# A three-level wavelet mix on one core: all products of TensorE on two halves of 64 rows, edge rows copied into one operand

## The chip, the core and the metric

The kernel runs on one core of a Trainium2 chip. The time is device time of one execution in microseconds; less is better. A core has TensorE (PE, matrix products into PSUM), VectorE (DVE), ScalarE (ACT), GpSimd (POOL) and SyncE (SP, which issues the DMAs here). They run their own instruction streams and meet at semaphores. SBUF and PSUM have 128 partitions; PSUM has 8 banks of 512 fp32 columns.

## What is computed

x is [8, 512, 207, 64] fp32: batch, time, nodes, channels. Each series of 512 steps is split by a three-level wavelet transform with 8 taps into four components, each component is multiplied by a weight of its channel, the transform is inverted, the 64 channels are mixed by a 64 x 64 matrix, and x and a bias are added:

```python
for _ in range(3):
    a, d = _dwt(a)                      # stride 2, 8 taps, along time
    details.append(d)
coeffs = [a] + details[::-1]
enh = [c * w[i] for i, c in enumerate(coeffs)]      # w[i]: one weight per channel
rec = enh[0]
for d in enh[1:]:
    rec = _idwt(rec[:, :d.shape[-1]], d)
return x + xr @ proj_w.T + proj_b       # xr: rec as [B, T, N, D]
```

## The kernel before

Time is cut into 4 windows of 128 steps, which lie on the partitions of `x_sb`. The three transforms of a window are one matrix: a window gives 128 coefficients of its own, and 20 more (`HALO_COLS`) reach over its edge and belong to the next window. The way back is a matrix too: a window's output needs its own 128 coefficients and the first 20 of the next window (its edge rows). After the last window there is a tail of 20 coefficients that no window owns.

Two nodes of 64 channels make a pair (128 rows or columns), four pairs a group (512 columns). 9 groups make a turn (`turn_of`), 23 turns all the nodes: 207 groups. The first and the last turn are written out, the 21 between run in a loop (`Fori`). Four slots of 18 nodes hold x; SP loads slot k+3 and stores slot k as the sums get done.

For each group the stages are:

- analysis (PE, `analyse`, L364), per pair: 4 products, one a window, with `x_sb` as the weights and the 148-column matrix moving, into the only set of banks `coefs_ps` (2 banks). Each needs the scaling of the pair before (`scaled`).
- scaling (DVE, `scale_pair`, L520): `coefs_ps` times the component weights to `coefs_sb`; POOL adds the 20 coefficients at the seam between windows 1 and 2 (`add_seam`, L311).
- projection (PE, `project`, L389), per window: 4 products, one a pair; the weights are 128 coefficients, the moving operand is `w_sb`, which holds the 64 x 64 matrix twice on its diagonal (128 x 128). Two banks `proj_ps` serve five tiles in turn: windows 0, 1, 2, the tail (`project_tail`, L396) and window 3.
- the split in two numbers of type fp32r: ACT copies the high part (`copy_high`, L493), DVE subtracts it for the low part (`split_low`, L526). The tail comes out transposed, is turned by DVE (`turn_tail`, L536, four instructions) and split by ACT (L498) and POOL (L316).
- synthesis (PE, `synthesise`, L407 to L409), per window: low matrix x high data, high x low, high x high, into its own bank of `synth_ps` (4 banks).
- edges (PE, `synthesise_edges`, L418): the edge rows are taken where they lie, in a block of 32 rows of the next window's tile. Coefficient orders (`OWN`, `ORDER_OF`) are chosen so that the blocks of the four windows are four different ones. Three steps of four products with 32 rows, which run side by side.
- bias and sum: POOL adds the bias to x (`add_bias`, L323), DVE adds the synthesis to it (`add_window`, L546).

PE's order is written out in its `turn_of`: projection of window 0, window 3 of the group behind, analysis of pair 0 of the group ahead, the edges of the group behind, then projection, analysis and synthesis by turns. fp32 products appear in the trace as two instructions each, with a weight load (PEld) each; fp32r products as one.

## Time and profile before

| | us |
|---|---|
| median of 3 runs (2462.97 to 2463.97) | 2463.24 |
| the profiled execution | 2463.63 |
| its span in the trace | 2461.8 |

| engine | busy us | share of the span |
|---|---|---|
| PE, matmuls | 2433.9 | 99% |
| PE, weight loads | 2203.3 | 89% |
| DVE | 1896.4 | 77% |
| POOL | 1473.9 | 60% |
| ACT | 626.5 | 25% |

Busy times of PE are modelled ends of pipelined matmuls: what a matmul costs is read from the distance of two starts, not from its duration. The granted clock of TensorE is 1.00 of 2.4 GHz in the stretches read below. DMA moved 435 MB at 177 GB/s. "<-" names what ended an engine's idle time; "issue" means nothing that the profile shows.

### The profile page before, as it was taken

Reading aid. Unit: us, or ns where it says so; the run is one execution under the profiler, and the core shown is the slowest. Engines: PE = TensorE matmul, PEld = TensorE weight load, DVE = VectorE, ACT = ScalarE, POOL = GpSimd, SP = SyncE. Lnnn points to the kernel's source line nnn. Section 1 sums busy time; section 2 is a strip of 40 time slices with the busy share of each in tenths; the row PEclk is TensorE's granted clock in tenths of the full one; section 3 lists DMA queues with packets and bytes.
Section 4 is the critical chain, followed back from the end, with each engine's and each line's share of the span. In section 5 each row is a group of like instructions: output and inputs, shape, how many; then the busy total and the mean of one; then the engine's idle time right before and its main releaser. Section 6 shows DMA issues by size and latency. Waiting matters only on the chain.

```text
span 2461.8 us, 51862 instructions
## 1 busy us (share of the span) xinstructions
PE 2433.9 (99%) x18630; PEld 2203.3 (89%) x18630; DVE 1896.4 (77%) x3315; ACT 626.5 (25%) x1038; POOL 1473.9 (60%) x1908
## 2 busy tenths in 40 slices
PE   7999999999999999999999999999999999999998
PEld 7999999999999999999999999999999989998987
DVE  4777777777777777777777777777777777777776
ACT  1222222222222222222222222222222222222222
POOL 4656665666656666665666666566665665666555
PEclk9999999999999999999999999999999999999999
DMA  3544454454544544454454544544454454644543
GB/s 129 200 174 179 173 197 153 168 216 153 222 162 153 204 173 177 171 195 153 172 211 153 227 157 153 208 174 177 170 192 157 172 207 153 230 154 153 212 162 128
DMA packets 106160, 435.35 MB, mean 177 GB/s; under 512 B 6288, under 2 KB 7696, under 8 KB 106128
## 3 DMA queue, kind: packets, MB, share of 16 engines
q1 hardware_dynamic: 105232, 434.13, 46.7%
q10 hardware_dynamic: 896, 0.79, 0.1%
q8 instruction: 20, 0.33, 0.1%
q14 instruction: 12, 0.10, 0.0%
HBM read 217.84 MB, written 217.06 MB: 177 GB/s over the span
## 4 chain that ended last, share of the span: by engine, by line
PE 98%; POOL 0%; issue 0%; DVE 0%; DMA 0%; ACT 0%; ACTq 0%; DVEq 0%; POOLq 0%
PE coefs_ps L364 34%; PE proj_ps L389 32%; PE synth_ps L409 8%; PE synth_ps L408 8%; PE synth_ps L407 8%; PE synth_ps L418 8%; PE proj_ps L396 2%; DMA comp_sb<-comp_w 0%; POOL scale_sb L301 0%; POOL tail_lo L316 0%; DVE x_sb L546 0%; DVE coefs_sb L520 0%; DVE proj_lo L526 0%; ACT proj_hi L493 0%; ACTq L166 0%
## 5 line engine op out<-in xcount | busy, mean ns | idle before, releaser
L323 POOL TENSOR_TENSOR x_sb<-x_sb,bias_sb 128x512 f32<-128x512 f32 x828 | 1052.7, 1271 | 5.2 <-issue 5.2
L364 PE MATMUL coefs_ps<-analysis_sb,x_sb 128*128 128x148 f32 x6624 | 975.3, 290 | 12.7 <-DMA analysis_sb<-analysis_m 9.1
L493 ACT ACTIVATE proj_hi<-proj_ps 128x512 fp32r<-128x512 f32 x828 | 494.6, 597 | 1807.1 <-PE proj_ps L389 1807.1
L389 PEld LDWEIGHTS proj_ps<-w_sb,coefs_sb 128*128 128x128 f32 x6624 | 835.3, 192 | 118.1 <-issue 82.8
L364 PEld LDWEIGHTS coefs_ps<-analysis_sb,x_sb 128*128 128x128 f32 x6624 | 895.6, 191 | 32.3 <-DMA analysis_sb<-analysis_m 9.1
L389 PE MATMUL proj_ps<-w_sb,coefs_sb 128*128 128x128 f32 x6624 | 897.5, 278 | 2.3 <-issue 1.6
L526 DVE TENSOR_TENSOR proj_lo<-proj_ps,proj_hi 128x512 fp32r<-128x512 f32 x828 | 573.0, 692 | 422.7 <-ACT proj_hi L493 408.9
L311 POOL TENSOR_TENSOR coefs_sb<-coefs_sb 128x20 f32<-128x20 f32 x828 | 187.2, 226 | 810.1 <-DVE coefs_sb L520 778.8
L520 DVE TENSOR_TENSOR coefs_sb<-coefs_ps,scale_sb 128x552 f32<-128x552 f32 x828 | 600.6, 725 | 86.8 <-PE coefs_ps L364 75.2
L546 DVE TENSOR_TENSOR x_sb<-synth_ps,x_sb 128x512 f32<-128x512 f32 x828 | 531.5, 684 | 32.4 <-PE synth_ps L418 29.7
L407 PE MATMUL synth_ps<-proj_hi,synthesis_lo 128*128 128x512 f32 x828 | 404.0, 488 | 0.7 <-DVE proj_lo L526 0.7
L316 POOL TENSOR_TENSOR tail_lo<-tail_sb,tail_hi 32x512 fp32r<-32x512 f32 x207 | 262.0, 1266 | 154.5 <-ACT tail_hi L498 151.3
L409 PE MATMUL synth_ps<-proj_hi,synthesis_hi 128*128 128x512 f32 x828 | 326.9, 395 | 0.0
L408 PE MATMUL synth_ps<-proj_lo,synthesis_hi 128*128 128x512 f32 x828 | 326.3, 394 | 0.0
L536 DVE STREAM_TRANSPOSE tail_sb<-proj_ps 32x128 f32<-32x128 f32 x828 | 259.6, 313 | 14.9
L409 PEld LDWEIGHTS synth_ps<-proj_hi,synthesis_hi 128*128 128x128 f32 x828 | 155.5, 188 | 35.6
L407 PEld LDWEIGHTS synth_ps<-proj_hi,synthesis_lo 128*128 128x128 f32 x828 | 157.7, 190 | 1.1 <-DVE proj_lo L526 1.1
L408 PEld LDWEIGHTS synth_ps<-proj_lo,synthesis_hi 128*128 128x128 f32 x828 | 157.7, 191 | 0.0
L498 ACT ACTIVATE tail_hi<-tail_sb 32x512 fp32r<-32x512 f32 x207 | 129.9, 628 | 5.2
L418 PE MATMUL synth_ps<-proj_hi,edge_lo 32*128 32x512 f32 x621 | 104.2, 497 | 1.3 <-POOL tail_lo L316 1.3
L418 PE MATMUL synth_ps<-tail_hi,edge_lo 32*128 32x512 f32 x207 | 102.7, 496 | 0.0
L396 PEld LDWEIGHTS proj_ps<-coefs_sb,w_sb 128*128 128x128 f32 x414 | 77.9, 188 | 19.1
(22 smaller groups left out, 644.5 us busy)
## 6 DMA issues: line engine op xcount, KB each, us to landing
out<-x_sb SPq DMA_DIRECT2D x184, 1152.0 KB, 6.0
x_sb<-x SPq DMA_DIRECT2D x182, 1152.0 KB, 11.2
x_sb<-x SPq DMA_DIRECT2D x1, 1024.0 KB, 9.6
x_sb<-x SPq DMA_DIRECT2D x1, 768.0 KB, 6.0
x_sb<-x SPq DMA_DIRECT2D x1, 512.0 KB, 4.2
bias_sb<-bias ACTq DMA_DIRECT2D x1, 256.0 KB, 6.9
analysis_sb<-analysis_m ACTq DMA_DIRECT2D x1, 222.0 KB, 7.0
synthesis_sb<-synthesis_m ACTq DMA_DIRECT2D x1, 192.0 KB, 6.9
```

The source lines that it names most:

```text
L316: nc.gpsimd.tensor_tensor(tail_lo[tail_rows, :], tail_sb[tail_rows, :], tail_hi[tail_rows, :].bitcast(fp32), ALU.subtract).then_inc(tail_l ...
L323: nc.gpsimd.tensor_tensor(cols, cols, bias_sb[:, :], ALU.add).then_inc(biased, 1)
L364: mm = nc.tensor.matmul(coefs_ps[:, w // PART_WINDOWS, AT[w]:AT[w] + COLS], x_sb[:, w, local * PAIR:(local + 1) * PAIR], analysis_sb[:, OR ...
L389: mm = nc.tensor.matmul(ps[:, p * PAIR:(p + 1) * PAIR], coefs_of(g, p)[:, own_cols(w)], w_sb[:, :], start=True, stop=True)
L407: nc.tensor.matmul(rec, lo, proj_hi[w][:, :], start=True, stop=False)
L408: nc.tensor.matmul(rec, hi, proj_lo[w][:, :], start=False, stop=False)
L409: nc.tensor.matmul(rec, hi, proj_hi[w][:, :], start=False, stop=False).then_inc(synthesised, 1)
L418: mm = nc.tensor.matmul(synth_ps[:, w, :], weight[rows, :], moving[w][rows, :], start=False, stop=step == 2)
L493: nc.scalar.activation(proj_hi[w][:, :], proj_ps[BANK[g][TILE_ORDER.index(w)]][:, :], ACT.Copy).then_inc(hi_copied, 1)
L520: nc.vector.tensor_tensor(coefs_of(g, p).rearrange("c (two k) -> c two k", two=PARTS)[:, :, 0:PART_COLS], coefs_ps[:, :, 0:PART_COLS], sca ...
L526: nc.vector.tensor_tensor(proj_lo[w][:, :], proj_ps[BANK[g][TILE_ORDER.index(w)]][:, :], proj_hi[w][:, :].bitcast(fp32), ALU.subtract).the ...
L546: nc.vector.tensor_tensor(cols, synth_ps[:, w, :], cols, ALU.add).then_inc(summed, 1)
```

## The change

A window is cut in two halves of 64 steps, and every product uses 64 of the array's 128 rows; products on the upper and the lower rows follow each other in pairs and write different banks.

- Analysis: 8 products per pair of nodes (4 windows x 2 halves), 64 rows, 84 columns. `analyse_first` has four, `analyse_second` the other four, which add to the same banks and wait for the first (`half_analysed`).
- Projection: one product per node instead of per pair: 64 rows (channels), 64 columns. Each node has its own bank; `proj_ps` is two tiles of two banks. The tail is two products into the free columns of window 3's tile.
- Synthesis: in units of two windows, (2, 3) and (0, 1), which share the two banks of `synth_ps`: `synthesise_first` has six products of 64 rows, `synthesise_second` six more and then the edges.
- Edges: ACT copies the 20 high and the 20 low edge rows of the next window to rows 0 and 32 of a half of `stack_sb` (`move_edge`, `move_tail`), where three rows hold the bias in three parts. Two steps (matrix low part, matrix high part) of two products with 64 rows take the place of three steps of four. The rows above the three bias rows in the matrix hold ones, so POOL's bias additions go away.
- The tail is turned by two transposes of 64 rows and split as 128 x 128 instead of 32 x 512.
- The orders of PE, DVE, ACT and POOL are rewritten; `add_window` waits for a unit (`synthesised`). At the start ACT splits the bias and issues 12 small DMAs into `stack_sb`.

```diff
@@ pe
+            def analyse_half(w, side, start, stop):
+                at = (w % PART_WINDOWS) * WINDOW + side * HALF
+                return lambda cols: nc.tensor.matmul(coefs_ps[:, w // PART_WINDOWS, at:at + HALF_COLS],
+                                                     x_sb[half_rows[side], w, cols], analysis_sb[half_rows[side], :],
+                                                     start=start, stop=stop, skip_group_check=True)
...
+                if not (first and local == 0):
+                    pe.wait_ge(scaled, (turn * GROUPS + g) * PAIRS + p)
+                cols = pair_cols(g, p)
+                analyse_half(0, 0, True, False)(cols)
+                analyse_half(2, 1, True, False)(cols)
+                analyse_half(1, 0, False, False)(cols)
+                analyse_half(3, 1, False, False)(cols).then_inc(half_analysed, 1)
+
+            def analyse_second(turn, g, p):
+                pe.wait_ge(half_analysed, (turn * GROUPS + g) * PAIRS + (p + 1))
+                cols = pair_cols(g, p)
+                analyse_half(2, 0, False, False)(cols)
+                analyse_half(0, 1, False, False)(cols)
+                analyse_half(3, 0, False, True)(cols)
+                analyse_half(1, 1, False, True)(cols).then_inc(analysed, 1)
...
+                for p in pairs:
+                    if w == ORDER[0]:
                         pe.wait_ge(seamed, group * PAIRS + (p + 1))
-                    mm = nc.tensor.matmul(ps[:, p * PAIR:(p + 1) * PAIR], coefs_of(g, p)[:, own_cols(w)], w_sb[:, :],
-                                          start=True, stop=True)
+                    for node in range(2):
+                        out_cols = proj_of(w)[:, node, 0:NODE_COLS].rearrange("k (h p c) -> k h p c", h=2, p=PAIRS)
+                        rows = node_rows[node]
+                        mm = nc.tensor.matmul(out_cols[:, :, p, :], coefs_of(g, p)[rows, own_cols(w)],
+                                              w_sb[rows, rows].rearrange("k (h c) -> k h c", h=2),
+                                              start=True, stop=True, skip_group_check=True)
...
+                for weight, stop in ((edge_lo[:, :], False), (edge_hi[:, 0, :], True)):
+                    nc.tensor.matmul(synth_ps[1][:, :], weight[half_rows[0], :], stack_sb[u][half_rows[0], :],
+                                     start=False, stop=stop, skip_group_check=True)
+                    mm = nc.tensor.matmul(synth_ps[0][:, :], weight[half_rows[1], :], stack_sb[u][half_rows[1], :],
+                                          start=False, stop=stop, skip_group_check=True)
+                mm.then_inc(synthesised, 1)
...
+                    if not start:
+                        synthesise_second(*behind, LATE)
+                    first_ahead(0)
+                    project(turn, g, 2, [0, 1, 2, 3], first)
+                    second_ahead(0)
+                    project(turn, g, 3, [0, 1, 2, 3], first)
+                    project_tail(g)
+                    first_ahead(1)
+                    if not start:
+                        synthesise_first(*behind, EARLY, [0, 1, 2], False)
+                    second_ahead(1)
+                    if not start:
+                        synthesise_second(*behind, EARLY)
+                    first_ahead(2)
+                    project(turn, g, 0, [0, 1, 2, 3], first)
+                    second_ahead(2)
+                    project(turn, g, 1, [0, 1, 2, 3], first)
...
+                    synthesise_first(turn, g, LATE, [0], first)
+                    first_ahead(3)
+                    synthesise_first(turn, g, LATE, [1, 2], first)
+                    second_ahead(3)
@@ act
+            def move_edge(turn, g, w, u, half, first):
+                group = turn * GROUPS + g
+                act.wait_ge(lo_copied, group * WINDOWS + (PLACE[w] + 1))
+                if not (first and g == 0):
+                    act.wait_ge(synthesised, group * 2 + (u - 1))
+                for at, source in ((HIGH_AT, proj_hi[w]), (LOW_AT, proj_lo[w])):
+                    rows = slice(half * HALF + at, half * HALF + at + HALO_COLS)
+                    nc.scalar.activation(stack_sb[u][rows, :], source[0:HALO_COLS, :].bitcast(fp32),
+                                         ACT.Copy).then_inc(edge_moved[w], 1)
...
+                    for q in range(4):
+                        cols = slice(q * PAIRS * QUAD, (q + 1) * PAIRS * QUAD)
+                        nc.scalar.activation(stack_sb[LATE][at:at + HALO_COLS, cols],
+                                             source[q * QUAD:q * QUAD + HALO_COLS, :].bitcast(fp32),
+                                             ACT.Copy).then_inc(tail_moved, 1)
...
+                    if not (first and g == 0):
+                        move_edge(*behind, 2, EARLY, 0, first and g == 1)
+                        move_edge(*behind, 1, EARLY, 1, first and g == 1)
+                    copy_high(turn, g, 2, first)
+                    copy_high(turn, g, 3, first)
+                    move_edge(turn, g, 3, LATE, 1, first)
+                    copy_tail_high(turn, g, first)
+                    move_tail(turn, g, first)
+                    copy_high(turn, g, 0, first)
+                    copy_high(turn, g, 1, first)
@@ dve
+                    if not (first and g == 0):
+                        split_low(*behind, 1)
+                    add_behind(2)
+                    add_behind(3)
                     scale_ahead(0)
+                    split_low(turn, g, 2)
+                    split_low(turn, g, 3)
+                    scale_ahead(1)
+                    turn_tail(turn, g, first)
                     add_behind(0)
                     add_behind(1)
                     scale_ahead(2)
+                    split_low(turn, g, 0)
                     scale_ahead(3)
```

## Rows read from the trace of the kernel before

**Rows 1.** The page, part 1: busy us, share of the span, instructions.

```profile
PE 2433.9 (99%) x18630; PEld 2203.3 (89%) x18630; DVE 1896.4 (77%) x3315; ACT 626.5 (25%) x1038; POOL 1473.9 (60%) x1908
```

**Rows 2.** The page, part 4: the chain that ended last, by line.

```profile
PE coefs_ps L364 34%; PE proj_ps L389 32%; PE synth_ps L409 8%; PE synth_ps L408 8%; PE synth_ps L407 8%; PE synth_ps L418 8%; PE proj_ps L396 2%; DMA comp_sb<-comp_w 0%; POOL scale_sb L301 0%; POOL tail_lo L316 0%; DVE x_sb L546 0%; DVE coefs_sb L520 0%; DVE proj_lo L526 0%; ACT proj_hi L493 0%; ACTq L166 0%
```

**Rows 3.** Waits of PE: total us, times, longest us.

```profile
PE coefs_ps L364 <- DVE coefs_sb L520: 3.7, 3, 1.9
```

**Rows 4.** Groups of instructions: PE's two fp32 lines; busy us, mean ns, idle before.

```profile
L364 PE MATMUL coefs_ps<-analysis_sb,x_sb 128*128 128x148 f32 x6624 | 975.3, 290 | 12.7 <-DMA analysis_sb<-analysis_m 9.1
L389 PE MATMUL proj_ps<-w_sb,coefs_sb 128*128 128x128 f32 x6624 | 897.5, 278 | 2.3 <-issue 1.6
```

**Rows 5.** Weight loads in order of time: start us, length us, line, count.

```profile
37.87 0.82 PEld L364 LDWEIGHTS coefs_ps<-analysis_sb,x_sb 128*128 128x128 f32 x6
38.84 0.19 PEld L418 LDWEIGHTS synth_ps<-proj_hi,edge_lo 32*128 32x128 f32 x3 [0.15 <-issue]
...
38.95 0.19 PEld L418 LDWEIGHTS synth_ps<-proj_lo,edge_hi 32*128 32x128 f32 x3
...
39.18 0.19 PEld L418 LDWEIGHTS synth_ps<-proj_hi,edge_hi 32*128 32x128 f32 x3
...
39.74 0.97 PEld L389 LDWEIGHTS proj_ps<-w_sb,coefs_sb 128*128 128x128 f32 x8 [0.37 <-issue]
40.63 1.06 PEld L364 LDWEIGHTS coefs_ps<-analysis_sb,x_sb 128*128 128x128 f32 x8
...
41.75 0.19 PEld L408 LDWEIGHTS synth_ps<-proj_lo,synthesis_hi 128*128 128x128 f32 x1
41.98 0.19 PEld L409 LDWEIGHTS synth_ps<-proj_hi,synthesis_hi 128*128 128x128 f32 x1
...
109.98 0.30 PEld L389 LDWEIGHTS proj_ps<-w_sb,coefs_sb 128*128 128x128 f32 x2 [0.37 <-issue]
```

**Rows 6.** Groups of instructions of the other engines, as in the fourth group.

```profile
L493 ACT ACTIVATE proj_hi<-proj_ps 128x512 fp32r<-128x512 f32 x828 | 494.6, 597 | 1807.1 <-PE proj_ps L389 1807.1
L526 DVE TENSOR_TENSOR proj_lo<-proj_ps,proj_hi 128x512 fp32r<-128x512 f32 x828 | 573.0, 692 | 422.7 <-ACT proj_hi L493 408.9
L520 DVE TENSOR_TENSOR coefs_sb<-coefs_ps,scale_sb 128x552 f32<-128x552 f32 x828 | 600.6, 725 | 86.8 <-PE coefs_ps L364 75.2
L546 DVE TENSOR_TENSOR x_sb<-synth_ps,x_sb 128x512 f32<-128x512 f32 x828 | 531.5, 684 | 32.4 <-PE synth_ps L418 29.7
L536 DVE STREAM_TRANSPOSE tail_sb<-proj_ps 32x128 f32<-32x128 f32 x828 | 259.6, 313 | 14.9
L498 ACT ACTIVATE tail_hi<-tail_sb 32x512 fp32r<-32x512 f32 x207 | 129.9, 628 | 5.2
L323 POOL TENSOR_TENSOR x_sb<-x_sb,bias_sb 128x512 f32<-128x512 f32 x828 | 1052.7, 1271 | 5.2 <-issue 5.2
...
L483 ACT ACTIVATE edge_hi<-edge_sb 128x128 fp32r<-128x128 f32 x1 | 0.3, 292 | 0.0
```

**Rows 7.** Analysis to scaling, scaling to analysis: PE and DVE in order of time.

```profile
1209.06 1.17 PE L364 MATMUL coefs_ps<-analysis_sb,x_sb 128*128 128x148 f32 x8
...
1210.27 0.73 DVE L520 TENSOR_TENSOR coefs_sb<-coefs_ps,scale_sb 128x552 f32<-128x552 f32 x1 [0.30 <-PE coefs_ps L364]
...
18.94 0.73 DVE L520 TENSOR_TENSOR coefs_sb<-coefs_ps,scale_sb 128x552 f32<-128x552 f32 x1 [2.49 <-PE coefs_ps L364]
...
19.73 2.34 PE L364 MATMUL coefs_ps<-analysis_sb,x_sb 128*128 128x148 f32 x8 [0.82 <-DVE coefs_sb L520]
```

**Rows 8.** DMA queues, and PE's first matmuls of the last turn in time order.

```profile
q1 hardware_dynamic: 105232, 434.13, 46.7%
...
q8 instruction: 20, 0.33, 0.1%
...
2346.85 0.40 PE L418 MATMUL synth_ps<-proj_hi,edge_hi 32*128 32x512 f32 x3
2347.87 0.39 PE L418 MATMUL synth_ps<-tail_hi,edge_hi 32*128 32x512 f32 x1 [0.62 <-issue]
```

More of the change, by code:

```diff
@@ L32 @@
 GROUP = PAIRS * PAIR
-TAIL = WINDOWS
-TILE_ORDER = [0, 1, 2, TAIL, 3]
-TILES = len(TILE_ORDER)
-TAIL_QUAD = 2
+NODE_COLS = GROUP // 2
+ORDER = [2, 3, 0, 1]
+PLACE = [ORDER.index(w) for w in range(WINDOWS)]
+UNITS = [(2, 3), (0, 1)]
+LATE, EARLY = 0, 1
+HIGH_AT, LOW_AT = 0, QUAD
+BIAS_AT = HALO_COLS
+BIAS_PARTS = 3
 SLOTS = 4
@@ new lines, in products, with synthesise_first @@
+            def products(u):
+                low, high = UNITS[u]
+                return [(synthesis_lo, proj_hi[low], proj_hi[high]), (synthesis_hi, proj_lo[low], proj_lo[high]),
+                        (synthesis_hi, proj_hi[low], proj_hi[high])]
+            def synthesise_first(turn, g, u, steps, first):
+                group = turn * GROUPS + g
+                if steps[0] == 0:
+                    pe.wait_ge(lo_copied, group * WINDOWS + (2 * u + 2))
+                    if not (first and g == 0 and u == 0):
+                        pe.wait_ge(summed, group * WINDOWS + 2 * u)
+                for step in steps:
+                    weight, low, high = products(u)[step]
+                    nc.tensor.matmul(synth_ps[0][:, :], weight[half_rows[0], :], low[half_rows[0], :],
+                                     start=step == 0, stop=False, skip_group_check=True)
+                    mm = nc.tensor.matmul(synth_ps[1][:, :], weight[half_rows[1], :], high[half_rows[1], :],
+                                          start=step == 0, stop=False, skip_group_check=True)
+                if steps[-1] == 2:
+                    mm.then_inc(half_synthesised, 1)
@@ L450, in turn_of @@
-                    project(turn, g, 2, first)
-                    analyse_ahead(2)
-                    synthesise(turn, g, 1, first)
-                    project_tail(turn, g, first)
-                    project(turn, g, 3, first)
-                    analyse_ahead(3)
-                    synthesise(turn, g, 2, first)
+                    start = first and g == 0
+                    behind = (turn, g - 1) if g > 0 else (turn - 1, GROUPS - 1)
+                    ahead = (turn, g + 1) if g + 1 < GROUPS else (turn + 1, 0)
@@ L485, in copy_high @@
+            act.wait_ge(rest_built, 2)
+            act.wait_ge(cleared, 2)
+            for u in range(2):
+                for half in range(2):
+                    for part in range(BIAS_PARTS):
+                        row = half * HALF + BIAS_AT + part
+                        act.dma_start(stack_sb[u][row:row + 1, :].bitcast(fp32),
+                                      bias_parts[:, part, :].bitcast(fp32)).then_inc(stacks_set, 16)
             def copy_high(turn, g, w, first):
                 group = turn * GROUPS + g
-                act.wait_ge(projected, group * TILES + (TILE_ORDER.index(w) + 1))
+                act.wait_ge(projected, group * WINDOWS + (PLACE[w] + 1))
@@ new lines, in move_tail @@
+            def move_tail(turn, g, first):
+                group = turn * GROUPS + g
+                act.wait_ge(tail_hi_copied, group + 1)
+                if not (first and g == 0):
+                    act.wait_ge(synthesised, group * 2 - 1)
+                for at, source in ((HIGH_AT, tail_hi), (LOW_AT, tail_lo)):
+                    if source is tail_lo:
+                        act.wait_ge(tail_lo_copied, group + 1)
+                    for q in range(4):
[3 more added lines that the diff above has]
+                                             ACT.Copy).then_inc(tail_moved, 1)
@@ L500, in turn_of @@
             def turn_of(turn, first=False):
                 for g in range(GROUPS):
-                    for w in range(WINDOWS):
-                        copy_high(turn, g, w, first)
-                    copy_tail_high(turn, g)
+                    behind = (turn, g - 1) if g > 0 else (turn - 1, GROUPS - 1)
+                    if not (first and g == 0):
+                        move_edge(*behind, 2, EARLY, 0, first and g == 1)
+                        move_edge(*behind, 1, EARLY, 1, first and g == 1)
```

403 lines of the change are left out of this document (189 added, 214 removed).

## Prediction

> **What bounds the kernel now.** I read four views, in this order. The page's first part [rows 1] has TensorE (PE) busy for 99% of the span and the weight loads (PEld) for 89%, DVE for 77%, POOL for 60%, ACT for 25%. The chain that ended last [rows 2] is PE for nearly all of the span: 34% analysis (L364), 32% projection (L389), four times 8% synthesis and edges. The waits [rows 3] confirm it: the longest entry of PE on DVE is 3.7 us in all, so in the steady loop PE waits for nobody. Only what PE itself executes counts, until something else takes 11.7 us for a group. The work repeats 207 times (23 turns of 9 groups); the first load of projection weights stands at 39.74 us and six groups later at 109.98 [rows 5], so a group takes 70.24/6 = 11.71 us. 207 x 11.71 = 2424 us, and 38 us are start and end.
>
> **What a product costs.** Each fp32 product is two instructions with a weight load each: 6624 records of L364 are 207 x 32 for 16 products [rows 4]. Eight loads of L389 last 0.97 us, each 0.19, so they start (0.97-0.19)/7 = 0.111 us apart; those of L364 (1.06-0.19)/7 = 0.124. The fp32r products with 512 columns follow each other at 0.23 (41.75 to 41.98) [rows 5]. L364 moves 148 columns and L389 128: at the price per column of the first (0.84 ns) the second would take 0.107, and it takes 0.111. What holds it there stands in the edge rows: the loads of the first step start at 38.84, those of the second at 38.95 although their matmuls start only 0.23 later. So a load of 128 weight columns occupies its rows for 0.11 us, with 32 rows as with 128, and the loads of four row groups run side by side [rows 5]. That is the term on which the forecast turns: dividing the array in two lets two matmuls and two loads run at once, but no load gets shorter, and one step of both halves can't be shorter than a load.
>
> **The change on PE, for a group.** Now: 32 x 0.125 (L364) = 4.0; 34 x 0.111 (L389 and the tail) = 3.8; 12 x 0.232 = 2.8; edges 3 x 0.235 = 0.7, with 0.21 us ahead of them (last load of L364 at 37.87+0.82-0.19 = 38.50, next 38.84, instead of 0.125 on) and 0.20 behind (38.84 to 39.74 is 0.90, minus 0.70) [rows 5]. Together 11.7, as measured. The last 0.4 is the price of going from 128 rows to 32 and back.
> After: analysis has 32 products of 84 columns, 64 instructions, 32 in each half. Projection has 32 products of 64 columns, 64 instructions. The tail has 4. By columns an analysis step would take 84 x 0.84 = 0.071 and a projection step 0.054; both are below the load's 0.11. So all 66 pair steps cost a load. I take 0.114: the two passes of one product stand next to each other on the same half, so the halves run shifted by one load and something is lost in step; bounds 0.108 (38.84 to 38.95) and 0.12. 66 x 0.114 = 7.5. Synthesis has 12 pair steps and the edges 4 (before 12 and 3): 16 x 0.232 = 3.7, bounds 0.226 and 0.235. The change of array shape and its 0.4 are gone. Sum 11.24 us, against 11.71: 0.35 off analysis and 0.41 off the switching, 0.1 more on projection and 0.23 more for the fourth edge step (0.03 is rounding).
>
> **Does something else become late?** DVE: four scalings (0.725), four low splits (0.692), four additions (0.684) stay; four transposes of 32 rows become two of 64 (0.313 each if 64 rows run like 32, 0.63 if not). Page sum 1896/207 = 9.2 minus 0.6 = 8.5 us [rows 1, 6]: below 11.2, so hidden; reading the additions in runs of 32 columns and the splits from two banks I cost at nothing for that reason, up to 2.7 us a group are free. POOL loses the four bias additions (1.27 us each) and keeps seams and a shorter tail split: no bound. ACT gains most: per group four copies of 0.6, six moves of edge rows with 20 x 512 elements (nearest row tail_hi, 32x512: 0.63), one copy of the tail and eight moves of 128 columns (nearest row, edge_hi 128x128: 0.29): 2.4 + 3.8 + 2.6 = 8.8 us, in order [rows 6]. Its place matters: the moves of window 3 wait for DVE's split of it, the tail moves for the transposes; the copy of window 0 is queued behind both, and DVE's split of window 0 and its last scaling behind that. With PE's order at 11.24 us I get (from the start of the late second synthesis) split of 3 done at 5.6, moves to 6.9, transposes done at 7.2, nine tail copies to about 9.8, copy of window 0 to 10.4, its split to 11.1, and the last scaling is due at 11.4. 0.3 us to spare by unoverlapped durations; the tail's moves are due at PE at 11.9.
> The tightest loop is the single set of analysis banks. A first analysis waits for the scaling of the pair before. Last matmul to scaling 0.33 (1209.06+1.17-0.29 = 1209.94 to 1210.27), scaling 0.73, to PE 0.06 (18.94+0.73 to 19.73), and a load of 0.11 before the first matmul: 1.23, some 0.05 less for a shorter matmul [rows 7]. Between them the change puts at least projection 3 and the tail, ten steps: 1.14 + 0.11 = 1.25. So it just fits; a stall of 0 to 0.05 four times a group is in the range and not in the sum. Where the analysis was the cover before, this cover is gone if a step gets shorter than 0.11.
> **The loop's code.** In the last turn, whose code PE meets for the first time, one of four equal matmuls starts at 2347.87 and the three before it at 2346.85, with "issue" as the reason: 1.0 us. PE's instruction queue moved 20 packets, 0.33 MB, in the whole run [rows 8]: that is the first turn, the loop body and the last turn, once each, at 0.11 MB for 9 x 180 = 1620 instructions and their waits. So 21 passes of the body were served without a new fetch. The new body has 9 x 328 = 2952, some 0.20 MB. Whether that still stays is not to be seen in this trace; bounds: nothing, and 1.0 us for each 16 KB packet, 13 a turn. I take one such stall a turn, as at the loop's exit: 21 us.
> The Trainium skill (Runtime: NRT & Kernel Launch, Instruction fetch mechanics) gives PE room for 2048 instructions and says that a jump out of the window held waits for a fetch; no run here shows that limit, and by it the new body doesn't fit where the old one did.
> Start and end: twelve small DMAs and their splits must land before the first synthesis: +3 us (0 to 8). Loads and stores of x don't change; DMA engines are busy for 47% [rows 8].
>
> **Sum.** 207 x 11.24 = 2327, + 38 + 3 + 21 = 2389 span, + 1.8 us outside it (2463.6 against 2461.8 now) = 2391; the profiled execution is 0.4 us above the median, so 2390. Own range: 10.74 us a group and no fetches give 2265; 11.9 with stalls and two fetches a turn give 2545.
>
> **Rivals.**
> A. Loads aren't the floor: two loads of a half overlap, or 64 rows load faster. Then steps cost their columns, 32 x 0.071 + 32 x 0.054 + 2 x 0.107 + 3.7 = 7.9 us; the analysis banks' loop adds about 1 us (1.2 instead of 0.7 behind two of the four pairs) and DVE (8.5) and ACT (8.8) are as long, so about 9.2: 207 x 9.2 + 62 = 1970. Against it: 0.11 in the edge rows, and 0.111 where the columns ask 0.107; for it: no row has a matmul shorter than a load.
> The Trainium skill (TensorEngine Tiling (Array Packing), Theoretical Speedup) promises up to 2x for a contraction of 64 rows or fewer; this is that rule, and by the trace it holds for 512 columns but not for 64.
> B. Slower, by code fetching: every packet of the body is fetched anew each turn and PE waits for it: 13 x 1.0 x 21 = 273 us on 2369: 2640. For it: 1.0 us at a first meeting. Against it: the first turn's code came without such stalls. It decides from (2463-2369)/21 = 4.5 us a turn.
> C. The change doesn't do what it says on fp32: the halves take turns, because the two passes of a product stand together and the load of the other half isn't drawn ahead of them. A step then costs up to two loads, 0.222: 66 x 0.108 more, +1475, 3870. Rows show side-by-side loads only for fp32r with one pass. Slower from 0.120 a step on.
>
> **How the numbers follow.** Likeliest case 0.62, of it 0.50 faster, 0.03 within 0.2%, 0.09 slower (a step of 0.12 or two and more fetches a turn); A 0.16; B 0.12; C 0.10. Faster 0.66, same 0.03, slower 0.31; 0.2% is about what a measurement of this kernel tells from no change. The range takes in A and the likeliest case and leaves out B and C: 1950 to 2560.
>
> **What the new profile would show.** Groups 11.2 us apart; loads of one half 0.11 us apart in analysis and projection, loads of the other between them; no idle around the edges; DVE at 73 to 77% of the span, ACT near 75%, POOL under 20%; packets of PE's instruction queue: 20 to 40 if the body stays, near 290 if not. Waits of PE on the scaling (L520's successor) of more than 0.1 us a group would make the loop of the analysis banks the bound; loads of a half under 0.1 us apart speak for A, over 0.2 for C.

## The result, and the profile after

The changed kernel takes 2435.14 us (median of 6 runs, 2427.27 to 2450.86) against 2462.92 us before (2462.56 to 2463.97): a ratio of 0.9889, 95% interval 0.9857 to 0.9922. It is faster, by 27.8 us where the prediction has 73. The profiled execution took 2432.38 us, its span is 2430.5, so 31.3 us less than the span before.

The first part of its page, the two queues and the chain that ended last, in the columns of [rows 1, 2, 8]:

```profile
PE 2357.3 (97%) x33948; PEld 2200.8 (91%) x33948; DVE 1752.8 (72%) x2906; ACT 1830.6 (75%) x3938; POOL 290.8 (12%) x1111
...
q1 hardware_dynamic: 105232, 434.13, 47.4%
q8 instruction: 296, 4.85, 0.8%
...
PE 96%; issue 2%; DVE 1%; POOL 0%; ACTq 0%; DMA 0%; ACT 0%; DVEq 0%
```

ACT went from 25% to 75%, POOL from 60% to 12%, DVE from 77% to 72%; PE fell from 99% to 97%, and "issue" now has 2% of the chain: time in which PE waited for nothing that the profile shows. PE's instruction queue (q8) moved 296 packets, [rows 8] had 20. The groups of instructions:

```profile
L602 DVE TENSOR_TENSOR coefs_sb<-coefs_ps,scale_sb 128x552 f32<-128x552 f32 x828 | 604.7, 730 | 253.3 <-PE coefs_ps L340 237.8
L534 ACT ACTIVATE proj_hi<-proj_ps 128x512 fp32r<-128x512 f32 x828 | 471.9, 596 | 218.3 <-PE proj_ps L400 160.0
...
L552 ACT ACTIVATE stack_sb<-proj_hi 20x512 fp32r<-20x512 f32 x621 | 390.8, 629 | 214.1 <-DVE proj_lo L609 209.0
...
L565 ACT ACTIVATE stack_sb<-tail_hi 20x128 fp32r<-20x128 f32 x828 | 255.1, 308 | 21.8
```

The edge moves of 20 rows take 629 and 308 ns, about what 32 and 128 rows took in [rows 6] (628 and 292). How far apart the groups are is read from an operation that each does once. DVE's transposes of the tail, two groups in a row:

```profile
503.96 0.63 DVE L620 STREAM_TRANSPOSE tail_sb<-proj_ps 64x128 f32<-64x128 f32 x2
...
515.15 0.63 DVE L620 STREAM_TRANSPOSE tail_sb<-proj_ps 64x128 f32<-64x128 f32 x2
```

Over all 206 distances the median is 11.186 us (before 11.71). 206 x 0.524 = 108 us are won. Yet the span is only 31 shorter: the distances add up to 65 us more than 206 times their median (before: 0.5), and what lies before the first transpose and behind the last grew by 12. The waits of PE and PEld (total us, times, longest us) say where:

```profile
PEld coefs_ps L340 <- DVE coefs_sb L602: 63.5, 181, 11.0
...
PE synth_ps L431 <- issue: 29.3, 20, 2.2
...
PEld proj_ps L390 <- issue: 10.5, 18, 0.9
```

L431 is the first product of a turn. Twenty times PE has no work in front of it, by 1.5 us on average (0.9 to 2.2): these are the 20 jumps back to the start of the loop's body, since its 21st pass falls through. Eighteen times a load of L390 waits as well, by 0.6 us on average; sixteen of these waits stand 4.3 to 5.1 us ahead of such a jump, in the last group of the body. Both in one turn:

```profile
859.35 0.44 PE L390 MATMUL proj_ps<-w_sb,coefs_sb 64*128 64x64 f32 x5 [0.76 <-issue]
...
863.93 0.49 PE L431 MATMUL synth_ps<-proj_hi,synthesis_lo 64*128 64x512 f32 x1 [1.19 <-issue]
```

The longest wait at a jump, with what follows it:

```profile
342.57 0.58 PE L340 MATMUL coefs_ps<-analysis_sb,x_sb 64*128 64x84 f32 x8
...
345.34 0.18 PEld L431 LDWEIGHTS synth_ps<-proj_hi,synthesis_lo 64*128 64x128 f32 x1 [2.35 <-issue]
345.35 0.50 PE L431 MATMUL synth_ps<-proj_hi,synthesis_lo 64*128 64x512 f32 x1 [2.20 <-issue]
...
347.44 1.83 PEld L390 LDWEIGHTS proj_ps<-w_sb,coefs_sb 64*128 64x128 f32 x16
```

Sixteen loads take 1.83 us here. In the steady loop they take 0.98 (first row of the next fence but one). The table of stretches (us, busy us and instructions of PE, PEld, DVE, ACT, POOL, granted clock, DMA share, GB/s) has the reason, first for this place, then for an undisturbed one:

```profile
338.70:349.90 11.20, 9.00 (x112) 8.52 (x112) 5.57 (x10) 6.73 (x17) 1.02 (x4) 0.84 0.36 146
...
1344.90:1356.10 11.20, 11.20 (x168) 10.35 (x168) 8.44 (x15) 8.84 (x20) 1.36 (x5) 1.00 0.78 287
```

After the idle 2.2 us the granted clock fell from 2.4 to 1.2 GHz at 346.4, for 10.2 us; the same happened at 1483.0 and 2001.8, about 4.4 us lost each time, and for 3.4 us at 240.5. The spread of the six runs goes with it: the two at 2427 and 2428 us have a mean granted clock of 0.992, the one at 2451 has 0.982. So up to 61 us of the 65 are the loop's (the other 4 are the first group's).

The steady loop itself, PE's weight loads in order of time:

```profile
333.39 0.98 PEld L390 LDWEIGHTS proj_ps<-w_sb,coefs_sb 64*128 64x128 f32 x16
334.28 0.53 PEld L340 LDWEIGHTS coefs_ps<-analysis_sb,x_sb 64*128 64x128 f32 x8
334.73 0.98 PEld L390 LDWEIGHTS proj_ps<-w_sb,coefs_sb 64*128 64x128 f32 x16
```

Sixteen and eight loads, 12 pair steps, take 334.73 - 333.39 = 1.34 us: 0.1115 a step, although analysis moves 84 columns and projection 64. Synthesis and edges follow each other at 0.2325. 66 x 0.1115 + 16 x 0.2325 = 11.08 us, and 0.106 is missing to the 11.186.

Last the start. POOL, DVE and ACT's DMA queue, in order of time:

```profile
8.06 9.22 POOL L296 COPY scale_sb<-comp_sb 128x6 f32<-128x6 f32 x72 [7.62 <-DMA comp_sb<-comp_w]
...
17.32 0.73 DVE L602 TENSOR_TENSOR coefs_sb<-coefs_ps,scale_sb 128x552 f32<-128x552 f32 x1 [15.08 <-POOL scale_sb L296]
...
30.21 7.64 ACTq L524 DMA_DIRECT2D stack_sb<-bias_parts  x12
...
37.90 1.08 ACT L534 ACTIVATE proj_hi<-proj_ps 128x512 fp32r<-128x512 f32 x2 [8.43 <-issue]
```

The first scaling starts at 17.32 (before: 12.54, then [rows 7] at 18.94 for the third), since the component weights now have 72 pieces for POOL to copy where they had 41. And ACT issues the twelve bias DMAs ahead of its first copy. The first transposes stand at 40.37, before at 33.83.

And the end, where 5 of the 12 us lie. The two units of synthesis share two banks, so in the last group the first product of the early unit waits until DVE's additions for the late one (L629, 2416.27 to 2417.55) are done:

```profile
2417.70 0.47 PE L419 MATMUL synth_ps<-proj_hi,synthesis_lo 64*128 64x512 f32 x1 [2.49 <-DVE x_sb L629]
```

### The profile page after: what moved, and what is told of

Its sections match the earlier page's. It is cut to its first block, busy times and chain, and to the rows that moved or that the text cites. A ratio compares the mean times of both kernels' runs of the same rounds, so it can differ in the third digit from the quotient of the medians.

```text
span 2430.5 us, 85182 instructions
## 1 busy us (share of the span) xinstructions
PE 2357.3 (97%) x33948; PEld 2200.8 (91%) x33948; DVE 1752.8 (72%) x2906; ACT 1830.6 (75%) x3938; POOL 290.8 (12%) x1111
## 3 DMA queue, kind: packets, MB, share of 16 engines
q8 instruction: 296, 4.85, 0.8%
## 4 chain that ended last, share of the span: by engine, by line
PE 96%; issue 2%; DVE 1%; POOL 0%; ACTq 0%; DMA 0%; ACT 0%; DVEq 0%
PE coefs_ps L340 30%; PE proj_ps L390 30%; PE synth_ps L419 11%; PE synth_ps L431 10%; PE synth_ps L442 6%; PE synth_ps L433 3%; PE proj_ps L400 2%; PE synth_ps L421 2%; PE synth_ps L444 2%; POOL scale_sb L296 0%; ACTq L524 0%; DMA comp_sb<-comp_w 0%; DVE coefs_sb L602 0%; DVE proj_lo L609 0%; DVE x_sb L629 0%
## 5 line engine op out<-in xcount | busy, mean ns | idle before, releaser
L340 PEld LDWEIGHTS coefs_ps<-analysis_sb,x_sb 64*128 64x128 f32 x13248 | 956.8, 189 | 120.9 <-DVE coefs_sb L602 63.5
L340 PE MATMUL coefs_ps<-analysis_sb,x_sb 64*128 64x84 f32 x13248 | 1017.3, 271 | 23.6 <-DVE coefs_sb L602 18.1
L390 PE MATMUL proj_ps<-w_sb,coefs_sb 64*128 64x64 f32 x13248 | 878.8, 272 | 8.1 <-issue 7.7
L390 PEld LDWEIGHTS proj_ps<-w_sb,coefs_sb 64*128 64x128 f32 x13248 | 821.4, 190 | 10.6 <-issue 10.5
L629 DVE TENSOR_TENSOR x_sb<-synth_ps,x_sb 128x512 f32<-128x512 f32 x828 | 531.6, 684 | 44.9 <-PE synth_ps L444 38.5
L552 ACT ACTIVATE stack_sb<-proj_hi 20x512 fp32r<-20x512 f32 x621 | 390.8, 629 | 214.1 <-DVE proj_lo L609 209.0
L552 ACT ACTIVATE stack_sb<-proj_lo 20x512 fp32r<-20x512 f32 x621 | 390.5, 629 | 15.2
L565 ACT ACTIVATE stack_sb<-tail_hi 20x128 fp32r<-20x128 f32 x828 | 255.1, 308 | 21.8
L431 PE MATMUL synth_ps<-proj_hi,synthesis_lo 64*128 64x512 f32 x414 | 200.0, 483 | 29.5 <-issue 29.3
L419 PE MATMUL synth_ps<-proj_hi,synthesis_lo 64*128 64x512 f32 x414 | 197.7, 478 | 2.7 <-DVE x_sb L629 2.7
L433 PE MATMUL synth_ps<-proj_hi,synthesis_lo 64*128 64x512 f32 x414 | 199.6, 482 | 0.0
L421 PE MATMUL synth_ps<-proj_hi,synthesis_lo 64*128 64x512 f32 x414 | 198.1, 478 | 0.0
L421 PE MATMUL synth_ps<-proj_lo,synthesis_hi 64*128 64x512 f32 x414 | 179.7, 434 | 0.0
L419 PE MATMUL synth_ps<-proj_lo,synthesis_hi 64*128 64x512 f32 x414 | 179.7, 434 | 0.0
L421 PE MATMUL synth_ps<-proj_hi,synthesis_hi 64*128 64x512 f32 x414 | 163.2, 394 | 0.0
L419 PE MATMUL synth_ps<-proj_hi,synthesis_hi 64*128 64x512 f32 x414 | 163.1, 394 | 0.0
```

The lines of the kernel that those rows point to most:

```text
L340: return lambda cols: nc.tensor.matmul(coefs_ps[:, w // PART_WINDOWS, at:at + HALF_COLS], x_sb[half_rows[side], w, cols], analysis_sb[half ...
L390: mm = nc.tensor.matmul(out_cols[:, :, p, :], coefs_of(g, p)[rows, own_cols(w)], w_sb[rows, rows].rearrange("k (h c) -> k h c", h=2), star ...
L419: nc.tensor.matmul(synth_ps[0][:, :], weight[half_rows[0], :], low[half_rows[0], :], start=step == 0, stop=False, skip_group_check=True)
L421: mm = nc.tensor.matmul(synth_ps[1][:, :], weight[half_rows[1], :], high[half_rows[1], :], start=step == 0, stop=False, skip_group_check=True)
L431: nc.tensor.matmul(synth_ps[1][:, :], weight[half_rows[0], :], high[half_rows[0], :], start=False, stop=False, skip_group_check=True)
L552: nc.scalar.activation(stack_sb[u][rows, :], source[0:HALO_COLS, :].bitcast(fp32), ACT.Copy).then_inc(edge_moved[w], 1)
```

## Experiments

Unless said otherwise a kernel differs from the changed one (2435.14) by the edit shown, and ratios are against the kernel before, which took 2463.2 to 2463.8 us beside each.

**The loop's code: does the closing branch cost the time?** PE's 21 turns written out one after the other:

```diff
-            with nc.Fori(1, TURNS - 1, engines=(ENG.PE,), hint_back_edge=True) as turn:
-                turn_of(turn)
+            for turn in range(1, TURNS - 1):
+                turn_of(turn)
```

> The changed kernel with PE's 21 loop passes written out one behind the other; every product stays. Theory J (the jump back to a loop body that no longer fits costs PE 2.1 to 2.3 us a turn, and in some turns the clock falls behind it): no jumps are left, though as much code is fetched, so 21 x 2.2 = 46 us go, and with them up to 14 us of half clock: 2375 to 2390 us, no start-to-start gap over 1.5 us at turn starts. Theory V (the amount of code fetched is what PE waits for, 296 packets): as much code, so 2430 to 2440.

Measured: 2376.98 us (2375.17 to 2377.39), ratio 0.965 [0.9634, 0.9666]. The queue's row and the same stretch as above:

```profile
q8 instruction: 270, 4.42, 0.7%
```
```profile
1344.90:1356.10 11.20, 11.20 (x168) 10.46 (x168) 8.40 (x15) 8.80 (x20) 1.33 (x6) 1.00 0.24 99
```

Nearly as much code is fetched as in the loop (4.42 MB, not 4.85), and PE hardly waits for it: the distances exceed their median, 11.186 as in the loop form, by 7.8 us in all and not by 65. So it isn't the amount fetched that costs time but the loop: the jump back and, in most turns, the wait just ahead of it. Theory J holds, V is wrong.

Three turns in the body, so 6 jumps for 21 turns where there were 20 (the last pass falls through; the expectation counts 7):

```diff
-            with nc.Fori(1, TURNS - 1, engines=(ENG.PE,), hint_back_edge=True) as turn:
-                turn_of(turn)
+            with nc.Fori(1, TURNS - 1, 3, engines=(ENG.PE,), hint_back_edge=True) as turn:
+                for ahead_turns in range(3):
+                    turn_of(turn + ahead_turns)
```

> The changed kernel with three turns in one pass of PE's loop: 7 jumps instead of 21, the same products. Theory J: 14 x 2.2 = 31 us go and two thirds of the clock's share: 2390 to 2405 us. Theory V: 2430 to 2440.

Measured: 2383.99 (2382.07 to 2385.29), ratio 0.9679 [0.9662, 0.9695], 7.0 us above the written-out form: 1.2 us a jump. The loop of one turn pays (2435.14 - 2376.98)/20 = 2.9 a jump: not only are there fewer jumps, each is shorter, which the expectation didn't have. The waits:

```profile
PE synth_ps L431 <- issue: 3.3, 6, 0.6
```

The same edit in the kernel before, whose body then no longer fits where one turn did:

> The kernel before with three turns in one pass of PE's loop: the body grows from 0.11 to 0.33 MB, past the 0.20 MB of the changed kernel; the products are the same. Theory J: 7 jumps (one fewer each time the last falls through) at 2.2 us: +13 to +16, about 2477 us, at most 2490 with clock drops. Theory W (the gap at the turn's start is a wait of the new order of stages, no code): 2463, no change.

Measured: 2470.84 (2468.61 to 2474.37), ratio 1.003 [1.002, 1.0039]: 7.4 us slower, about half of what was expected, and the gaps are there. One of six (0.7 to 2.1 us), with the row ahead of it:

```profile
1082.46 0.40 PE L409 MATMUL synth_ps<-proj_hi,synthesis_hi 128*128 128x512 f32 x1
...
1084.72 1.15 PE L389 MATMUL proj_ps<-w_sb,coefs_sb 128*128 128x128 f32 x8 [1.86 <-issue]
```

Nothing of the new products is in this kernel, so the stall belongs to the size of the body. W is wrong. The queue moved 159 packets here, where one turn in the body had 20 in all. And the converse, the kernel before with PE written out:

> The kernel before with PE's 21 loop passes written out. Theory J (its body was held, so its jumps cost next to nothing): 0.05 us a turn and the 1.0 us at the loop's exit go, 2460 to 2463 us. Rival (writing out by itself makes PE faster, in this kernel too): under 2450.

Measured: 2461.31 (2460.79 to 2461.73), ratio 0.9992 [0.9983, 1.0002]. 1.9 us less, of which 1.0 is the wait at the loop's exit [rows 8]: the old body was held, its jumps cost nothing that can be told.

Where the loop starts in PE's stream of code, first at the start of a block, then 140 instructions into one:

```diff
-            with nc.Fori(1, TURNS - 1, engines=(ENG.PE,), hint_back_edge=True) as turn:
+            with nc.Fori(1, TURNS - 1, engines=(ENG.PE,), hint_back_edge=True, head_slot={ENG.PE: 0}) as turn:
```

> The changed kernel with the head of PE's loop placed at the start of a fetched block of code, nothing else changed. Theory J1 (the jump waits because the block with the head holds only its last few instructions and the next block comes late): the gap at the turn's start falls under 1 us: 2395 to 2415 us. Theory J2 (the head's block is no longer held when the jump comes, wherever it starts): gap stays at 2 us, 2430 to 2440.

Measured: 2491.12 (2480.95 to 2512.47), ratio 1.0099 [1.0061, 1.0138]. Slower than either theory had it; J1 and J2 both fall.

> The changed kernel with the head of PE's loop in the middle of a fetched block (place 140 of 256) instead of at its start (which gave 2491) or where it falls by itself (2435). Theory P (what a jump costs hangs on where head and closing branch lie in their blocks): another gap again at the turn's start, between 0.5 and 3.5 us, total 2390 to 2490 but not within 3 us of 2435. Theory Q (any forced placement costs, by the branch that skips the padding or by what the loader adds): 2480 to 2500 as with place 0.

Measured, two runs: 2392.81 (2392.68 and 2392.93), ratio 0.9712 [0.9684, 0.974]. P holds. Last the loop as it was, without the hint that the branch is taken (`hint_back_edge=True` left out):

> The changed kernel without the instruction at the loop's head that names the jump ahead of time. Theory H (the naming saves part of the fetch, but not all): the gap grows from 2 us to 3 to 5 us, 2455 to 2500. Theory N (it does nothing for a body this long): 2430 to 2440.

Measured, two runs: 2540.24 (2536.17 and 2544.31), ratio 1.031 [1.0271, 1.035]: H in direction, more than it expected. One row of waits and the span with its mean granted clock, for slot 0, slot 140 and no hint (there with the queue's row):

```profile
PE synth_ps L431 <- issue: 55.9, 21, 3.4
...
core 0: 2510.6 us, clock 0.960
```
```profile
PE synth_ps L431 <- issue: 10.3, 17, 0.8
```
```profile
PE synth_ps L431 <- issue: 65.4, 20, 3.6
...
q8 instruction: 315, 5.16, 0.8%
...
core 0: 2534.3 us, clock 0.961
```

The same body, the same number of jumps: 0.6, 1.5, 2.7 and 3.3 us of idle at each (10.3/17, 29.3/20, 55.9/21, 65.4/20; at slot 0 the loop's entry is the 21st). In the two long cases the granted clock falls to the lower level at most jumps (15 of 21 at slot 0 and 16 of 20 without the hint, for 10 to 14 us), with 0.6 us at none, nor with the three turns in the body. That is why the price per turn, (2491.12 - 2376.98)/21 = 5.4 and (2540.24 - 2376.98)/21 = 7.8 us, is twice the gap and more. Without the hint the queue moved 19 packets more than with it (296), about one a jump; what they hold isn't shown.

**The step: is it the load?** Zeros widen the analysis matrix from 84 to 120 moving columns:

```diff
+WIDE_COLS = 120
...
-                return lambda cols: nc.tensor.matmul(coefs_ps[:, w // PART_WINDOWS, at:at + HALF_COLS],
+                return lambda cols: nc.tensor.matmul(coefs_ps[:, w // PART_WINDOWS, at:at + WIDE_COLS],
```

> The changed kernel with 120 moving columns in each analysis product instead of 84; the added 36 columns of the matrix are zeros. Theory L (a step of both halves lasts as long as a weight load, 0.111 to 0.114 us; 120 columns ask only 120 x 0.84 ns = 0.101): groups stay 11.19 us apart, 2427 to 2451 us in all. Theory C (steps cost their columns and something else takes the rest): 32 x 0.030 = 0.97 us more a group, near 2630.

Measured, one run: 2436.47 us, groups 11.223 us apart. L holds. Two rows of its loads:

```profile
1201.04 0.57 PEld L341 LDWEIGHTS coefs_ps<-analysis_sb,x_sb 64*128 64x128 f32 x8
1201.49 1.02 PEld L391 LDWEIGHTS proj_ps<-w_sb,coefs_sb 64*128 64x128 f32 x16
```

Eight loads in 0.45 us, 0.1125 a step: 43% more columns in 32 of the steps cost 0.04 us a group.

**The order of the halves.** Two products of the upper rows, then two of the lower, in place of turns:

```diff
                 analyse_half(0, 0, True, False)(cols)
-                analyse_half(2, 1, True, False)(cols)
                 analyse_half(1, 0, False, False)(cols)
+                analyse_half(2, 1, True, False)(cols)
                 analyse_half(3, 1, False, False)(cols).then_inc(half_analysed, 1)
```

and likewise in `analyse_second`.

> The changed kernel with the four products of each half analysis sorted by half of the array: two on the upper rows, then two on the lower, instead of by turns. Theory O (weight loads start in the order written, and a load waits until its half has begun the matmul before): four loads of one half follow each other at 0.11 before the other half gets its first, so eight loads take 0.67 to 0.78 us instead of 0.46, eight times a group: 13.0 to 13.8 us a group, 2800 to 2970 us. Theory F (loads of the other half are drawn ahead freely): 11.19 a group, near 2435.

Measured, one run: 2457.7 us, groups 11.287 apart: 0.10 us a group more. Had four loads of one half held up the other half, 1.8 to 2.6 us would have been added a group; O is wrong, F nearly right. 206 x 0.101 = 20.8 us are nearly all of the 22.6 between the two times. In the group looked at, most of the 0.10 shows in one place, the early unit's second synthesis and edges: there the lower half runs one load behind the upper (L431 at 1203.43, L433 at 1203.54, where the changed kernel starts both at 1201.03), and from the analysis load ahead of it to the one behind it are 1.73 us (1202.87 to 1204.60) for 1.64 (1200.46 to 1202.10).

**The edges before.** The kernel before without its twelve edge products, and without PE's wait for the tail ahead of them; `synthesised` takes the place of `completed`:

```diff
-                for step, (weight, moving) in enumerate(((edge_lo, source_hi), (edge_hi, source_lo),
-                                                         (edge_hi, source_hi))):
-                    for w in range(WINDOWS):
...
-                        mm = nc.tensor.matmul(synth_ps[:, w, :], weight[rows, :], moving[w][rows, :],
-                                              start=False, stop=step == 2)
```

> The kernel before without its edge products: the 12 products with 32 rows are left out, so the output lacks the contribution of the next window's coefficients. Theory M (going to blocks of 32 rows and back costs 0.41 us a group beside the three steps): 11.71 - 1.11 = 10.60 us a group, 2232 us. Rival: only the three steps go, 0.70, and the idle stays with the fp32 and fp32r neighbours: 11.0 a group, 2315.

Measured, one run: 2276.75 us, groups 10.808 apart, so 0.90 less: between the two. With the edges gone only projection 0 lies between the last analysis of a group and the first of the next:

```profile
1207.30 0.99 PEld L389 LDWEIGHTS proj_ps<-w_sb,coefs_sb 128*128 128x128 f32 x8
1207.62 0.73 DVE L511 TENSOR_TENSOR coefs_sb<-coefs_ps,scale_sb 128x552 f32<-128x552 f32 x1 [0.30 <-PE coefs_ps L364]
...
1208.41 0.68 PEld L364 LDWEIGHTS coefs_ps<-analysis_sb,x_sb 128*128 128x128 f32 x5
```

The load of L364 waits for the scaling until 1207.62 + 0.73 + 0.06 = 1208.41 (so the 0.06 that the prediction read at 19.73 us, where the granted clock was still 1.2 GHz, holds at 2.4 GHz), where eight loads of 0.111 behind 1207.30 would have let it start at 1208.2. 0.90 and these 0.20 make 1.10, which is what the three edge steps with their 0.41 of switching came to in the prediction. It agrees with that figure but doesn't isolate it.

**The missing 0.106.** It is a wait for the scaling, once a group. In the written-out form, ACT, DVE and PEld in order of time:

```profile
1501.56 1.31 ACT L565 ACTIVATE stack_sb<-tail_hi 20x128 fp32r<-20x128 f32 x4
1502.89 1.31 ACT L565 ACTIVATE stack_sb<-tail_lo 20x128 fp32r<-20x128 f32 x4
1504.22 1.09 ACT L534 ACTIVATE proj_hi<-proj_ps 128x512 fp32r<-128x512 f32 x2
...
1504.85 0.69 DVE L609 TENSOR_TENSOR proj_lo<-proj_ps,proj_hi 128x512 fp32r<-128x512 f32 x1 [1.36 <-ACT proj_hi L534]
1505.46 0.72 DVE L602 TENSOR_TENSOR coefs_sb<-coefs_ps,scale_sb 128x552 f32<-128x552 f32 x1
...
1506.23 0.52 PEld L340 LDWEIGHTS coefs_ps<-analysis_sb,x_sb 64*128 64x128 f32 x8 [0.27 <-DVE coefs_sb L602]
```

ACT's copy of window 0 stands behind eight moves of the tail, DVE's split of window 0 waits 1.36 us for the copy, and the last scaling is queued behind that split; analysis of the next group is late. On top of the written-out form, the copy goes between the moves of the high part and those of the low part:

```diff
@@ move_tail
                 for at, source in ((HIGH_AT, tail_hi), (LOW_AT, tail_lo)):
+                    if source is tail_lo:
+                        copy_high(turn, g, 0, first)
@@ act's order
                     move_tail(turn, g, first)
-                    copy_high(turn, g, 0, first)
```

> The changed kernel, PE written out, and ACT's copy of window 0 moved ahead of the four moves of the tail's low part. Theory A (ACT's queue makes DVE's split of window 0 late, that makes the last scaling late by 0.26 us, and PE's first analysis load then stands open for 0.12 us): 0.12 x 207 = 25 us less than 2377, 2350 to 2355. Rival (the load at that place stands open anyway, or the tail's moves become late for the edges): 2370 to 2380.

Measured: 2351.16 (2350.44 to 2351.38), ratio 0.9544 [0.953, 0.9559]; groups 11.080 apart, which is 66 x 0.1115 + 16 x 0.2325 to the last digit. A holds. The same places:

```profile
1499.90 0.57 ACT L534 ACTIVATE proj_hi<-proj_ps 128x512 fp32r<-128x512 f32 x1
1500.49 1.31 ACT L567 ACTIVATE stack_sb<-tail_lo 20x128 fp32r<-20x128 f32 x4
1500.52 0.68 DVE L610 TENSOR_TENSOR proj_lo<-proj_ps,proj_hi 128x512 fp32r<-128x512 f32 x1
...
1502.39 0.73 DVE L603 TENSOR_TENSOR coefs_sb<-coefs_ps,scale_sb 128x552 f32<-128x552 f32 x1 [1.19 <-PE coefs_ps L340]
```
```profile
PEld coefs_ps L340 <- DVE coefs_sb L603: 16.9, 3, 11.0
```

The split no longer waits, the scaling waits for PE again, and the 183 waits of the load on it in the written-out form are 3. Of the 25.8 us gained, 206 x 0.106 = 21.8 are this; the other 4 weren't traced.

**The start.** On top of that, POOL copies both parts of `scale_sb` at once, and the three bias rows go in one DMA for each half of a stack (PE waits for 4 of them, not 12):

```diff
-            for part in range(PARTS):
-                for c, n, i in component_runs():
-                    last = nc.gpsimd.tensor_copy(scale_sb[:, part, c:c + n],
-                                                 comp_sb[:, i:i + 1].to_broadcast([PAIR, n]))
+            for c, n, i in component_runs():
+                last = nc.gpsimd.tensor_copy(scale_sb[:, :, c:c + n],
+                                             comp_sb[:, i:i + 1].to_broadcast([PAIR, PARTS, n]))
...
-                    for part in range(BIAS_PARTS):
-                        row = half * HALF + BIAS_AT + part
-                        act.dma_start(stack_sb[u][row:row + 1, :].bitcast(fp32),
-                                      bias_parts[:, part, :].bitcast(fp32)).then_inc(stacks_set, 16)
+                    row = half * HALF + BIAS_AT
+                    act.dma_start(stack_sb[u][row:row + BIAS_PARTS, :].bitcast(fp32),
+                                  bias_parts[:, :, :].bitcast(fp32)).then_inc(stacks_set, 16)
```

> As the one with the sooner copy, and a shorter start: POOL fills both parts of the scale in 36 copies instead of 72, and the bias rows go in 4 DMAs instead of 12. Theory S (72 copies take 9.2 us ahead of the first scaling, where 40 took 5.2 before, and the 12 DMA issues hold ACT for 7.6 us): 8 to 10 us less, 2342 to 2347. Rival (the start is covered by the loads of x): 2350 to 2355.

Measured: 2344.02 us (2342.7 to 2344.35), ratio 0.9516 [0.9503, 0.9529]. Its start:

```profile
7.86 4.87 POOL L295 COPY scale_sb<-comp_sb 128x12 f32<-128x12 f32 x36 [7.42 <-DMA comp_sb<-comp_w]
...
12.77 0.73 DVE L601 TENSOR_TENSOR coefs_sb<-coefs_ps,scale_sb 128x552 f32<-128x552 f32 x1 [10.53 <-POOL scale_sb L295]
...
25.66 2.97 ACTq L522 DMA_DIRECT2D stack_sb<-bias_parts  x4
...
31.95 0.63 DVE L619 STREAM_TRANSPOSE tail_sb<-proj_ps 64x128 f32<-64x128 f32 x2
```

The first transposes come 8.4 us sooner (31.95 for 40.37) and the kernel ends 7.1 us sooner. How much of it each of the two edits gave isn't shown. This is the version that beats both: the change with three edits takes 119 us off the kernel before, where it alone takes 28.

## Why the prediction was right in direction and wrong in size

**The bound and the floor: right.** PE stayed the bound, and one step of both halves costs one load. The price was taken too high: 0.114 for a loss by shifted halves, where the loads of the two halves run in step at 0.1115. That is 66 x 0.0025 = 0.16 us a group in the kernel's favour. Synthesis and edges at 0.232 were right (0.2325), and so was taking the 0.41 of switching off: without it the groups could not be 11.08 apart. The new edge steps run with no gap around them.

**"0.3 us to spare" on ACT and "it just fits": wrong by 0.11 us a group.** The prediction followed the right chain (tail moves, copy of window 0, its split, last scaling) and found 0.3 us of room from durations of rows [rows 6]. The durations were right, 8.84 us of ACT a group as against 8.8; the places were off. ACT begins the copy as its queue allows, and the split ends after the last analysis has. Both of its sums of an order came out with thin margins, 0.3 us here and 1.25 against 1.23 in the loop of the analysis banks, and a margin that thin should have been priced and not taken at nothing. 11.186 for 11.24 came out close only because this miss (+0.11) and the one above (-0.16) cancel.

**The loop's code: the step that failed.** The prediction took 21 us, one stall of 1.0 us a turn; it was up to 61 (58 by the written-out form), 2.8 us a turn. It left open whether the body is held; it isn't (296 packets, "near 290 if not"). That code in sequence comes in time was right. Wrong was the size of one stall. The only row that could price it was a first meeting of code that lies ahead [rows 8], not a jump back. A jump cost 0.9 to 2.2 us of idle, a second gap of 0.2 to 0.8 stood ahead of it in 16 of 20 turns, and three times the granted clock halved for 10 us, which no term had. Rival B had PE wait for every packet; the 270 packets of the written-out form refute that. At 4.5 us a turn, it said, the change turns slower. With 2.8 the change stayed ahead; with the loop's head at slot 0 (5.4) or without the hint (7.8) it was indeed slower than before.
The Trainium skill (Runtime: NRT & Kernel Launch, Instruction fetch mechanics) says that crossing a block boundary in sequence is mostly hidden and that a jump out of the window held waits for a fetch. The runs agree with both: the written-out form streams 270 packets nearly unnoticed, and the loop of the kernel before pays with a body of three turns and not with one. It also gives PE 128 KiB; 20 packets for three turns' code before are 6.7 of 16 KB for one (110 KB, held), 270 for 23 are 11.7 (190 KB, not held), which lies on either side of it. The two pages of 16 KB that it names as the window don't fit these rows: PE held 6.7.

**Start and end: +3 taken, +16 measured.** 12 at the ends and 4 in the first group. The prediction priced the landing of twelve DMAs and not their issue: ACT was held by it for 7.64 us (8.43 idle before its first copy), queued ahead of that copy. It didn't look at POOL's 72 copies at all, which put the first scaling 4.8 us later. Both are instructions of a changed step that hold up what is queued behind them. At the end the shared banks of the two units, which the prediction didn't price either, add a wait of 2.5 us for DVE's additions; nothing was tried there.

**In sum.** 206 x (11.186 - 11.71) = -108; code +61 and the first group +4, less the 0.5 that was there; ends +12: -31, where the spans differ by 31.3. The prediction had 207 x (11.24 - 11.71) = -97, +21 and +3. Of the 41 us between its span (2389) and the measured one (2430.5) the code is 40, start and end are 13, and the groups give 11 back. The range, 1950 to 2560, holds the measured time, but it is so wide that this says little.

**The other rivals.** A (steps cost their columns, 1970) is refuted by the loads 0.1115 apart and by 120 columns at the same price. C (the halves take turns, 3870) is refuted by the group itself, and, with two products of one half in a row, by the mere 0.10 us that this costs.

**What stays open.** What in the placement of the loop's head makes the gap 0.6, 1.5 or 2.7 us, and why three turns in a body have short ones; four settings don't make a rule. Why PE waits ahead of the jump too in 16 of 20 turns, where with the head at slot 0 a load of L390 waits once in the whole run. Whether leaving 32-row steps gave exactly 0.41. How the start's 7.1 us divide between POOL's copies and the DMAs.

## What to carry to other kernels

Dividing the array in row halves pays up to the weight load and no further: when the moving operand is shorter than the load (here 64, 84 and 120 columns in fp32), a step of both halves costs one load, whatever the columns. Before doubling the instructions of a loop, look at how many packets its instruction queue moves: a body that was held and no longer is pays at each jump back, and the cures are to write the turns out or to place the head. And an engine that takes over small moves needs its queue's order checked against who waits for what stands behind them; one copy moved in ACT's order was worth 25.8 us here.

## What the runs showed of the hardware that was not expected

- The same loop with the same code took 2392.8, 2435.1, 2491.1 or 2540.2 us depending on where its head lay and whether the jump was announced: 147 us between best and worst, with nothing else changed.
- A gap of 1.7 us or more in PE's work can cost more than itself: at 346.4 the granted clock went to the 1.2 GHz level 1.0 us after the work had begun again, and stayed there for 10.2 us, at a price of about 4.4. In no kernel here did the clock fall at a jump whose gap was shorter than 1.6 us, and not at every longer one (1.9 us at 555.3, and it stayed). In the last turn the clock also fell without such a gap, at 2380.7 for 3.4 us.
- 4.42 MB of instructions, each met once, stream beside 434 MB of data nearly unnoticed: all irregularities of the written-out form together are 7.8 us, 3.7 of them in the first group, and in the kernel before writing out costs nothing (0.9992).
- ACT copies of 20 rows cost about what copies of 32 or 128 do, 629 ns against 628 for 512 columns and 308 against 292 for 128: the price is in the columns.
